# Eight PSUM banks dealt out anew in a fused attention and mixture kernel

## The reference

```python
x = x + attn_a(layernorm(x))   # 16 heads of 8, rotary, causal
x = x + ffn(layernorm(x))
x = x + attn_b(layernorm(x))   # the same shape, other weights
x = x + ffn(layernorm(x))      # the same ffn

# attention: q, k, v projections, rotary on q and k
att = softmax(where(causal, q @ k.T / sqrt(8), -inf)); y = (att @ v) @ wp

# ffn: attention with 8 heads of 64 and no mask, mixed by 5 experts
v   = sum_e topk2(x @ Ws)_e * sigmoid(x @ Ws)_e * (x @ Wv[e])
out = sum_e topk2(x @ Wd)_e * ((softmax(q @ k.T / 8) @ v) @ Wo[e])
```

## Time and profile before

| | |
|---|---|
| median of 3 runs | 2080.2 us (2077.26 to 2080.99) |
| the profiled execution | 2074.39 us, its span 2072.6 us |
| a full iteration, from 876.07 to 994.86 us | 118.79 us |
| TensorE busy | 1816.3 us, 88% of the span |
| VectorE busy | 1580.1 us, 76% |
| ScalarE busy | 1273.3 us, 61% |
| GpSimd busy | 1047.0 us, 51% |
| granted TensorE clock, mean | 0.967 of full |

### The profile page before, as it was taken

How to read it: one execution, slowest core, us unless ns; L and a number is a source line. 1 busy time by engine, 2 the same in 40 slices (tenths; PEclk the granted TensorE clock), 3 DMA queues, 4 the chain that set the end, 5 groups by cost and what they waited for, 6 DMA issues and landing times.

```text
span 2072.6 us, 32651 instructions
## 1 busy us (share of the span) xinstructions
PE 1816.3 (88%) x11328; PEld 881.0 (43%) x11328; DVE 1580.1 (76%) x2934; ACT 1273.3 (61%) x2803; POOL 1047.0 (51%) x1124
## 2 busy tenths in 40 slices
PE   1658999989999898989999998999999899998775
PEld 0223443535444353535444453544435354443332
DVE  4538787888878788788888888887878888787461
ACT  0335757576675757566675756667575766758461
POOL 1223556363645646374655636465563636455433
PEclk8879999999999999999999999999999999999986
DMA  3231203112121302113120211213021121200000
GB/s 97 48 36 32 37 29 43 35 26 30 37 37 42 36 30 33 23 37 36 42 37 30 40 33 27 33 39 37 29 44 35 26 29 37 36 17 14 11 1 6
DMA packets 87617, 68.71 MB, mean 33 GB/s; under 512 B 10720, under 2 KB 83104, under 8 KB 87328
## 3 DMA queue, kind: packets, MB, share of 16 engines
q1 hardware_dynamic: 87456, 66.62, 17.5%
HBM read 32.51 MB, written 10.49 MB: 21 GB/s over the span
## 4 chain that ended last, share of the span: by engine, by line
PE 64%; DVE 13%; ACT 10%; POOL 6%; DMA 3%; issue 3%; SPq 0%; POOLq 0%; DVEq 0%; ACTq 0%; PEldq 0%
PE Y L463 11%; PE M L556 5%; POOL Z L1069 5%; PE S2a L428 5%; ACT Pq L683 5%; PE S1c L404 5%; PE S2b L428 4%; DVE nmaxF L848 4%; PE M L593 3%; PE S1b L404 3%; PE M L514 3%; PE M L489 3%; DMA Ks<-parts 3%; DVE ztmp L930 3%; PE Y L454 2%
## 5 line engine op out<-in xcount | busy, mean ns | idle before, releaser
L1069 POOL TENSOR_TENSOR Z<-Z,ztmp 128x1280 f32<-128x1280 f32 x112 | 324.5, 2897 | 327.9 <-DVE ztmp L958 326.8
L1036 POOL TENSOR_SCALAR_AFFINE_SELECT PT<-PT 128x256 f32<-128x256 f32 (+1 forms) x640 | 254.5, 409 | 386.6 <-ACT PT L668 383.5
L1060 POOL TENSOR_TENSOR Vf<-Vf,ztmp 128x512 f32<-128x512 f32 x256 | 349.0, 1363 | 102.2 <-DVE ztmp L930 93.6
L668 ACT ACTIVATE PT<-S2a 128x512 f32<-128x512 f32 x320 | 191.6, 599 | 170.6 <-PE S2a L422 166.2
L463 PE MATMUL Y<-PT,Vf 128*64 128x512 f32 x1024 | 274.8, 617 | 0.0
L672 ACT ACTIVATE PT<-S2a 128x512 f32<-128x512 f32 x256 | 153.6, 600 | 158.5 <-PE S2a L428 155.7
L930 DVE TENSOR_TENSOR ztmp<-xv,wv_s 128x512 f32<-128x512 f32 x256 | 238.0, 930 | 2.8 <-POOL Z L1069 2.8
L404 PE MATMUL S1c<-Kf,Qf 64*128 64x512 f32 x352 | 203.6, 659 | 36.2 <-ACT Pq L683 32.2
L404 PE MATMUL S1a<-Kf,Qf 64*128 64x512 f32 x352 | 204.5, 662 | 20.6 <-ACT Pq L683 20.6
L668 ACT ACTIVATE PT<-S2b 128x512 f32<-128x512 f32 x320 | 191.5, 598 | 26.3 <-PE S2b L422 26.0
L404 PE MATMUL S1b<-Kf,Qf 64*128 64x512 f32 x320 | 182.8, 652 | 9.5 <-ACT Pq L683 9.5
(11 more groups left out here) (108 smaller groups left out, 3760.7 us busy)
## 6 DMA issues: line engine op xcount, KB each, us to landing
Qs<-parts SPq DMA_DIRECT2D x96, 128.0 KB
Ks<-parts SPq DMA_DIRECT2D x96, 128.0 KB
tab_s<-in_tab SPq DMA_DIRECT2D x16, 512.0 KB, 4.5
xr<-out_x SPq DMA_DIRECT2D x32, 256.0 KB, 2.9
out_x<-res SPq DMA_DIRECT2D x32, 256.0 KB, 2.2
wa_s<-in_wa SPq DMA_DIRECT2D x16, 320.0 KB, 3.1
xl<-out_x SPq DMA_DIRECT2D x16, 256.0 KB, 3.0
out_x<-in_x SPq DMA_DIRECT2D x8, 256.0 KB, 4.4
```

The source lines that it names most:

```text
L668: nc.scalar.activation(PT[:, slot % 2, b, :], t[:, :], ACT.Exp, scale=SCALE_A).then_inc(exps_done.sem, 1)
L1036: last = nc.gpsimd.affine_select(out=v, in_=v, compare_op=ALU.is_ge, fill=0.0, base=0, pattern=pattern, channel_multiplier=-1)
L1060: nc.gpsimd.tensor_tensor(Vf[:, i, :, :], Vf[:, i, :, :], vtmp[:, n % VBUF, :, :], ALU.add).then_inc(v_acc.sem, 1)
L1069: nc.gpsimd.tensor_tensor(Z[:, :, :, :], Z[:, :, :, :], ztmp[:, hh % 2, :, :, :], ALU.add).then_inc(z_acc.sem, 1)
```

## The change

The eight banks are dealt out anew:

| | before | after |
|---|---|---|
| first pass, S1 | 3 | 4 |
| second pass, S2 | 2 | 2, with ScalarE's other tiles in turn between |
| Y | 1 | 1 |
| VectorE's and ScalarE's other tiles, M0 and M1 | 2 | none |
| VectorE's tiles, M | none | 1 |

`free_for` of a second-pass bank waits for the use two back in the new list `S2_USES`, whatever it is. `skip` waits for all uses before it in its list (`turn_of`). The second pass of a missing group is now skipped use by use. Some tiles move: A xnT from (2, 4) to (2, 5), A kp from (3, 4) to (3, 6), A out from (5, 4) to (5, 5), F out from (2, 1) to (2, 2) on TensorE; on VectorE the second and fourth rotation, A v, A out and F out one or two steps later.

```diff
-        S1 = [pb("S1a"), pb("S1b"), pb("S1c")]
+        S1 = [pb("S1a"), pb("S1b"), pb("S1c"), pb("S1d")]
         S2 = [pb("S2a"), pb("S2b")]
         Y = pb("Y")
-        M0, M1 = pb("M0"), pb("M1")
-        M0_USES = [...]
-        M1_USES = [...]
+        M = pb("M")
+        M_USES = ["YT6",
+                  "YT7",
+                  "YT0", "F out", "A q", "A qp",
+                  "YT1", "A k", "A kp",
+                  "YT2",
+                  "YT3", "A v", "A out",
+                  "YT4",
+                  "YT5"]
...
+        BETWEEN = {(0, 3): ("rows1",), (1, 3): ("rows2",), (2, 3): ("rows3",), (7, 3): ("rows0",), (1, 9): ("ZT0", "ZT1", "ZT2"),
+                   (2, 5): ("A xnT",), (5, 2): ("A yNT",), (6, 1): ("F xnT",), (6, 5): ("F gate0", "F gate1"),
+                   (6, 6): ("F gate2", "F gate3")}
+        for p, step in enumerate(F_STEPS):
+            BETWEEN[step] = (f"F q{p}", f"F k{p}")
+        S2_USES = []
+        for s in range(NS):
+            for b in range(STEPS):
+                if b < N_BANKS[s]:
+                    S2_USES.append((s, b))
+                S2_USES += BETWEEN.get((s, b), ())
...
+        def bank(k, use):
+            return M if use in M_USES else S2[(k * len(S2_USES) + S2_USES.index(use)) % len(S2)]
...
+        def free_for(k, use):
+            if use in M_USES:
+                return m_drained.sem, m_drained.at(k, M_USES.index(use))
+            return s2_drained.sem, s2_drained.at(k, S2_USES.index(use) + 1 - len(S2))
+
+        def turn_of(k, use):
+            uses, signal = (M_USES, m_drained) if use in M_USES else (S2_USES, s2_drained)
+            return signal.sem, signal.at(k, uses.index(use))
...
                 def skip(use):
-                    pe.wait_ge(*free_for(j, use))
+                    pe.wait_ge(*turn_of(j, use))
                     pe.sem_inc(is_full(use), 1)
                     pe.sem_inc(is_free(use), 1)
...
                 def pass2(slot, b):
-                    n = BEFORE2[slot] + b + 1
-                    t = S2[(n - 1) % len(S2)]
+                    use = (slot, b)
+                    t = bank(j, use)
                     if not (a if slot < SA else f):
-                        if b == 0:
-                            pe.wait_ge(exps_done.sem, exps_done.at(j, n - 1))
-                            pe.sem_inc(s2_filled.sem, N_BANKS[slot])
-                            pe.sem_inc(exps_done.sem, N_BANKS[slot])
-                        return
+                        return skip(use)
...
-                    pe.wait_ge(exps_done.sem, exps_done.at(j, n - len(S2)))
+                    pe.wait_ge(*free_for(j, use))
...
-                        if at == (2, 4):
+                        if at == (2, 5):
                             xn_transposes("A xnT", a_prep)
...
                         if at == (3, 4):
                             a_project("A k")
+                        if at == (3, 6):
                             a_project("A kp")
...
-                        if at == (5, 4):
+                        if at == (5, 5):
                             a_output()
...
-                        if at == (2, 1):
+                        if at == (2, 2):
                             f_output()
```

More of the change, by code:

```diff
@@ L429, in pass2 @@
                                                        ident[:, :])
-                    last.then_inc(s2_filled.sem, 1)
+                    last.then_inc(is_full(use), 1)
                 def has_values(slot):
@@ L458, in values @@
                         if kt == 0:
-                            pe.wait_ge(exps_done.sem, exps_done.at(j, BEFORE2[slot]))
+                            pe.wait_ge(*drained(j, (group, NF_B - 1), 0 if slot else 1))
                         if group == SA:
@@ L473, in rows @@
                     pe.wait_ge(*free_for(j, use))
-                    t = bank(use)
+                    t = bank(j, use)
                     pe.wait_ge(nmb_ready.sem, nmb_ready.at(j, group + 1, 1 if group else 0))
@@ L530, in a_y_transposes @@
                     pe.wait_ge(*free_for(j, "A yNT"))
-                    t = bank("A yNT")
+                    t = bank(j, "A yNT")
                     for i in range(NT):
@@ L541, in a_output @@
                     pe.wait_ge(*free_for(j, "A out"))
-                    t = bank("A out")
+                    t = bank(j, "A out")
                     for i in range(NT):
@@ L589, in f_output @@
                     pe.wait_ge(*free_for(j, "F out"))
-                    t = bank("F out")
+                    t = bank(j, "F out")
                     for i in range(NT):
@@ L690, in rows @@
                     act.wait_ge(rowsA_in.sem, rowsA_in.at(j, 2 * group, 1 if group else 0))
-                    drain(f"rows{group}", mrowA[:, :], bank(f"rows{group}")[:, :].bitcast(BF)[0:2 * GA * NT, 0:P])
+                    drain(f"rows{group}", mrowA[:, :], bank(j, f"rows{group}")[:, :].bitcast(BF)[0:2 * GA * NT, 0:P])
                 def part0(qk):
@@ L729, in iteration @@
                         if at == (5, 2) and a:
-                            drain("A yNT", yT[:, :], bank("A yNT")[:, :])
+                            drain("A yNT", yT[:, :], bank(j, "A yNT")[:, :])
                         if b == 3 and (slot + 1) % NS < SA:
@@ L813, in rotate @@
                     dve.wait_ge(*filled(j, use))
-                    nc.vector.scalar_tensor_tensor((rot, rot2)[half], bank(use)[:, :],
+                    nc.vector.scalar_tensor_tensor((rot, rot2)[half], bank(j, use)[:, :],
                                                    ba_s[:, 2 * qk + half:2 * qk + half + 1], tab_s[:, half, :],
@@ L878, in a_output @@
                     flat = res[:, :, :].rearrange("p t c -> p (t c)")
-                    nc.vector.tensor_tensor(flat, bank("A out")[:, :], flat, ALU.add).then_inc(resA_ready.sem, 1)
+                    nc.vector.tensor_tensor(flat, bank(j, "A out")[:, :], flat, ALU.add).then_inc(resA_ready.sem, 1)
                     dve.wait_ge(resA_ready.sem, resA_ready.at(j, 1, 1))
```

92 lines of the change are left out of this document (35 added, 57 removed).

## The result

The changed kernel takes 2088.8 us (median of 5 runs, 2087.54 to 2090.44), the kernel before 2080.2 us (5 runs, 2076.42 to 2083.93): 1.0044 times the time, with a 95% interval of 1.0027 to 1.0060. It is slower, by some 9 us; forecast were 2069.5 us, and a range up to 2088. The profiled executions lie further apart than the medians, 2086.4 against 2072.6 us of span, since that of before lies 5.8 us under its median.

What follows compares the result with a forecast made beforehand. TensorE is busy 88% of the span; in slots 3 and 4 three level engines wait for each other. Steady -22.5, iteration 17 -11, skips at the end +14.0, start +8.8: -10.7 us, from 2080.2 to 2069.5 us; range 2050 to 2088.

Steps and rivals of the forecast that it cites:

- the steady gain: Iterations 2 to 16: fewer bank waits less new ones, -1.5 us an iteration, -22.5 us for the 15.
- the limit behind slot 4: Transposes of Y wait for VectorE's chain through slot 4, so TensorE's 3 us lead there is taken as only -2.1 us.
- F out: Slot 2: its new place waits for group 0's division, mostly filled by a pair of score matmuls; +0.2 us an iteration.
- A qp: Slot 2: in the one bank M it waits for VectorE's read of A q; +0.44 us an iteration.
- A kp moves two steps back, to where its bank has just been read: One bank M: the moved A kp has its bank free on arrival, costed at nothing.
- The first rival: One bank makes VectorE's reads the limit: slower, 2102 or 2086 us, deciding from 0.71 us an iteration; chance 0.18.
- A out and the gates: Late in an iteration: A out costs nothing, third and fourth gates wait for ScalarE's copies, 0.2 us together.
- the clock falling more often: Rival about the granted clock, given a chance of 0.07; no term of the sum holds it.
- The second failed step: Iteration 17: 12.5 of 15.1 us of exponential waits taken back, less 1.5 us for skipped tiles: -11 us.
- the start: Before iteration 1: more skips make TensorE 5.8 us late at xn, plus waits for VectorE; +8.8 us together.
- the end: Behind the last matmul: second-pass uses skipped singly at 0.30 us; +14.0 us, 26 us of steps instead of 13.
- the scatter would not be the limit: Slots 3 to 6: its DMAs cost only hidden tenths; the rival with it as limit said 2084 us, chance 0.15.

Runs made afterwards that it cites:

- experiment 7: Changed kernel without skips (2049.0 us), with two of VectorE's seven value products moved from slot 4 to slot 5; 2033.2 us, 0.9791 of the kernel before.
- experiment 12: Experiment 11's kernel with a third value product moved from slot 4 to slot 5; 2008.1 us, 0.9665 of the kernel before.
- experiment 9: Changed kernel with two matmuls of no use run while TensorE waits for Z; 2083.1 us, 1.0028 of the kernel before.
- experiment 6: Changed kernel without skips (2049.0 us), with A qp and A kp and VectorE's reads of them one step later; 2029.2 us, 0.9773 of the kernel before.
- experiment 3: Changed kernel without any skip of a tile, semaphores counting only the tiles that are there; 2049.0 us, 0.9856 of the kernel before.
- experiment 4: Changed kernel with three first-pass banks, S1d taken away, skips kept; 2175.1 us, 1.0471 of the kernel before.
- experiment 11: Experiment 10's kernel with the wait for Z filled by two matmuls of no use; 2013.4 us, 0.9697 of the kernel before.
- experiment 1: Kernel before, its banks kept, with second-pass uses of an absent group counted up one by one instead of in one pair of steps; 2100.3 us, 1.0103.
- experiment 5: Changed kernel without skips (2049.0 us), with the three transposes of Z one step later and F out at (2, 3); 2048.2 us, 0.9856 of the kernel before.
- experiment 2: Kernel before, its banks kept, without any skip of a tile, semaphores counting only the tiles that are there; 2068.5 us, 0.9954.
- experiment 10: Changed kernel without skips, A qp and A kp one step later and two value products moved to slot 5; 2018.3 us, 0.9716 of the kernel before.

## Why the prediction was wrong

**The step that failed is the steady gain, -1.5 us an iteration, and in it above all the -2.1 us taken for the limit behind slot 4.** The gain was mis-sized at full clock (-0.46) and had nothing in it for the clock. In iterations 3 to 15 that is 17.4 us (-2.1 for -19.5): 13.5 for the size and 3.8 for the clock. As TensorE's shift against before in iteration 8 (negative is sooner):

| up to | forecast | measured |
|---|---|---|
| slot 3 begins | +0.15 | +0.69 |
| slot 4 begins | -1.25 | -0.86 |
| slot 5 begins | -2.95 | -2.97 |
| YT3 | -2.1 | -1.50 |
| behind A yNT | -1.7 | -1.09 |
| the end | -1.5 | -0.46 |

- *The limit behind slot 4* is the term that was mis-sized most: -2.1 was taken for it because VectorE has 11.6 us of work in the slot's 13.5, and -1.50 came. What sets it was named rightly, VectorE's chain up to the copy of Y. TensorE was 3.0 us ahead when slot 5 began, as forecast, and lost half of that in one wait, which shrinks when VectorE has less to do in slot 4 (experiments 7 and 12). A yNT behind it cost +0.41 for +0.4.
- *F out* cost +0.69 in slot 2 for the +0.2 forecast. The values behind it begin 32.75 us into the iteration (914.46 us, L458), for 32.06 before (908.13 us, L454), with the same distance up to YT0. It waits 0.35 us for VectorE's division, in every full iteration at full clock (in all 13 of experiment 9); in those with a fall TensorE comes too late to wait for it. The rest of slot 2 came as forecast: -0.43 for the two waits that go (-0.49) and +0.44 for A qp. By slot 5 the loss was made good; whether it delays VectorE's chain no run tells.
- *"A kp moves two steps back, to where its bank has just been read", at nothing:* it waits 0.35 us in each iteration. A qp's was forecast (0.44, measured 0.37 of waiting and 0.44 of shift). Not seen was that these tiles delay the chain that sets YT3: both moved by a step are worth 0.87 us an iteration (experiment 6). The first rival, one bank that makes VectorE's reads the limit, was right in its mechanism, with three of the six new neighbours (F out, A qp and A kp) waiting, and YT1, YT2 and A out not. Its threshold of 0.71 us counts what comes on top of A qp, which no run measures by itself.
- *A out and the gates:* between A yNT and YT4, where A out has its new place, TensorE lost +0.26; the gates and what follows cost +0.37; 0.2 was forecast in all. No experiment took these apart.
- *The clock:* 9 falls for 3. By the lengths at full clock, 1549.2 - 13 x 118.79 = 4.9 us of before and 1547.1 - 13 x 118.34 = 8.7 us of after are beyond them: +3.8 us. An iteration with a fall took 120.38 us for 118.79 before, 1.6 us more, and the chances give 0.07 to the clock falling more often. Less idle time did not mean fewer falls: the change brought TensorE's from 7.4 to 6.3 us an iteration, but the one wait behind which all nine falls come grew from 1.3 to 1.7 us. What an earlier TensorE wins ahead of that wait, it waits.

**The second failed step: 1.5 us in iteration 17 and nothing in 16 for lone skips.** By slot 5 iteration 17 was 13.4 us ahead, more than the 12.5 forecast (part of that is the clock's, 0.90 of full in this iteration for 0.83 before). The skips took 7.2 us back, and 2.6 in iteration 16 (experiment 3). I had priced a skip as two steps of a queue, 0.30 us; among real work its price is the depth of the ring, up to 2.1 us.

**Right:** the start (TensorE at xn at 33.95 us, 6.0 late for 5.8; the first score matmul at 75.45 us for 75; 8.4 us in all, where the terms of the prediction add up to 8.7 and not 8.8), the end (25.5 us of steps for 26, in all 10.9 for 14.0 us), the waits for exponentials, the new wait of A qp, and that the scatter would not be the limit (one wait of 0.2 us for it in 13 iterations). The steps of missing groups were indeed the dearest part of the change: 39.8 us with those that were there before.

**Open:** why one iteration has a fall and another with the same waits has none (iteration 10 of experiment 4 waits as the others do and runs at full clock), and why the wait before YT3, which is as long as the one for Z (1.67 us), never has a fall behind it; and how many falls the other executions of the kernel before have, of which no trace stands here. Experiments 9 and 11 separate the clock by their traces alone; the intervals of their times overlap those of the kernels without the filling.

## What to carry to other kernels

Give a pipeline's first and last iterations their own count of tiles rather than steps that keep a common count: the steps are work of the busiest queue (0.15 us each here, 13.2 us for the 88 that experiment 1 adds at the end), and a skip that waits for all that came before empties the ring around it (waits of up to 2.1 us in iteration 17). When a bank is freed for one pair of engines, look for the tile that now waits for the third, and move it by a step; its wait can delay that engine's chain too (here the two were worth 0.87 us an iteration, for 0.72 us of waits). And a wait of TensorE is not priced by its length alone: filling the 1.7 us wait for Z took all nine falls behind it away here (experiment 9), while moving it made another wait, of 2.4 us (experiment 5). The count of falls belongs in every comparison of two traces.

## What the runs showed of the hardware

- In these traces TensorE's wait for Z was followed, within 2 us of its end, by a fall of the granted clock from full to half for 3.4 us in some of the full iterations: behind the wait at 1.3 us in 2, 2 and 1 of 13 (the kernel before, experiments 1 and 2), at 1.7 us in 9, 11, 4, 9 and 6 of 13 (the changed kernel, experiments 3, 6, 7 and 10). Such a fall cost 0.5 to 1.6 us. The wait of 1.67 us before YT3 in the changed kernel had none behind it in any of the 13.
- In experiment 4, with waits of 1.3 and 2.0 us 7 us apart, the half clock lasted 10 to 14 us in eight of 13 iterations, 3.4 us in two, and did not come in three. It cost up to 6.4 us.
- Matmuls of no use, 1.6 us of them in a wait of 1.7 us, took all falls of the full iterations away (9 to 0 in experiment 9, 6 to 0 in experiment 11). The iteration at full clock took 118.34 us for 118.33, and 116.97 for 116.96.
- Steps of TensorE's queue that only handle semaphores, recorded with 51 ns each, followed each other at some 0.15 us: 49 skips in place of five pairs of steps, 88 steps more, added 13.2 us at the end of the kernel.
- In the traces of the kernel before and of the changed kernel all 11328 matmuls write to one of the eight banks. 2720 instructions of ScalarE and 1776 of VectorE name a bank as their input, and none of the 1124 of GpSimd and none of the DMAs does.
